# Two transformer blocks on one core: where the roots of the variances are taken, and what Pool does first in a stage

## The reference

```python
x = x + jnp.tanh(g_xattn[0]) * _L0_xattn_ref(_layernorm(x), ctx_512, ...)   # 16 heads over 361 latents, rotary
x = x + jnp.tanh(g_ffn[0])   * _L0_ffn_ref(_layernorm(x), ...)              # weights -1/0/1, rows quantised to 8 bits
x = x + jnp.tanh(g_xattn[1]) * _L1_xattn_ref(_layernorm(x), ctx_512, ...)   # causal, 16 heads
x = x + jnp.tanh(g_ffn[1])   * _L1_ffn_ref(_layernorm(x), ...)              # 7 routed experts (top 2) and a shared one

def _layernorm(x, axis=-1, eps=1e-05):
    m = jnp.mean(x, axis=axis, keepdims=True)
    v = jnp.var(x, axis=axis, keepdims=True)
    return (x - m) / jnp.sqrt(v + eps)
```

## Time and profile before

| | |
|---|---|
| median of 3 runs (lowest, highest) | 1941.34 us (1939.52, 1941.47) |
| the profiled execution | 1943.23 us, of which span 1941.4 us |
| granted PE clock, mean | 0.973 |
| PE busy | 1772.2 us, 91% |
| DVE busy | 1318.7 us, 68% |
| ACT busy | 913.6 us, 47% |
| Pool busy | 599.5 us, 31% |
| stage starts in the trace (first instruction) | 1033.88, 1214.70 and 1448.75 us |

### The profile page before, as it was taken

One profiled execution on the slowest core, in us unless ns is written; L12 is line 12 of the kernel. 1 busy time (PEld: TensorE's weight loads), 2 busy tenths in 40 slices (PEclk: granted clock), 3 DMA queues, 4 the chain that ended last, 5 costly groups with the idle time before them and its releaser, 6 DMA issues. The chain is left out here.

```text
span 1941.4 us, 30474 instructions
## 1 busy us (share of the span) xinstructions
PE 1772.2 (91%) x10896; PEld 1408.2 (73%) x10910; DVE 1318.7 (68%) x2912; ACT 913.6 (47%) x2005; POOL 599.5 (31%) x582
## 2 busy tenths in 40 slices
PE   5899999999899999999996998799978989999997
PEld 4677887778777887778773544566655878888896
DVE  6677677776687778887777896477666633444564
ACT  3544445433543445434543554555544324555563
POOL 5332222331633122321211131232231454343353
PEclk9899999999999999999998999799989999999999
DMA  5022112210121222222205111000005167787773
GB/s 212 17 89 86 55 48 73 89 60 33 62 83 37 97 77 71 71 97 85 77 17 206 36 40 39 25 1 2 1 14 178 57 191 220 239 279 269 236 238 77
DMA packets 49671, 188.50 MB, mean 97 GB/s; under 512 B 7388, under 2 KB 11612, under 8 KB 38260
## 3 DMA queue, kind: packets, MB, share of 16 engines
q1 hardware_dynamic: 39396, 166.86, 24.0%
q0 software_dynamic: 9840, 19.70, 5.6%
q10 hardware_dynamic: 288, 0.00, 0.0%
HBM read 158.29 MB, written 28.24 MB: 96 GB/s over the span
## 5 line engine op out<-in xcount | busy, mean ns | idle before, releaser
L437 POOL TENSOR_TENSOR la_q_roped<-la_q_roped 128x400 f32<-128x400 f32 x128 | 134.7, 1074 | 655.8 <-DVE la_q_roped L968 655.8
L861 ACT ACTIVATE la_probs<-banks,la_minus_max 100x361 f32<-100x361 f32 x256 | 144.7, 565 | 176.6 <-DVE la_minus_max L1079 176.6
L968 DVE TENSOR_TENSOR la_q_roped<-banks,la_rope_q 128x400 f32<-128x400 f32 x384 | 198.0, 566 | 35.4 <-PE banks L552 26.6
L606 PEld LDWEIGHTS banks<-identity,la_probs 100*121 100x121 f32 x768 | 111.8, 185 | 79.4 <-DVE la_probs L1086 54.0
L1086 DVE TENSOR_SCALAR la_probs<-la_probs,la_rsum 100x361 f32<-100x361 f32 x256 | 153.9, 601 | 9.1
L645 PE MATMUL banks<-la_ctx_parts,la_wout_high 128*128 128x416 f32 (+3 forms) x512 | 157.9, 360 | 2.2 <-DVE residual L1020 1.9
L606 PE MATMUL banks<-identity,la_probs 100*121 100x100 f32 x768 | 128.2, 276 | 31.3 <-DVE la_probs L1086 18.9
L1079 DVE TENSOR_REDUCE la_minus_max<-banks 100x1 f32<-100x361 f32 x256 | 134.8, 526 | 29.9 <-PE banks L597 27.8
L617 PE MATMUL banks<-la_probs_t,la_kv_rows 121*128 121x200 f32 x768 | 152.4, 334 | 0.0
L2370 DVE TENSOR_TENSOR ex_weights_low<-ex_raw_weights,ex_weights_high 128x2048 fp32r<-128x2048 f32 x39 | 89.4, 2292 | 90.1 <-ACT ex_weights_high L2254 90.1
L879 ACT COPY la_probs_t<-banks 121x300 f32<-121x300 f32 x256 | 104.8, 409 | 64.0 <-PE banks L606 63.7
(11 more groups left out here) (378 smaller groups left out, 5017.1 us busy)
## 6 DMA issues: line engine op xcount, KB each, us to landing
ex_raw_weights<-w_exp SPq DMA_DIRECT2D x39, 1024.0 KB
la_weights<-w_pack SPq DMA_DIRECT2D x15, 1856.0 KB, 8.4
residual<-w_exp SPq DMA_DIRECT2D x24, 1024.0 KB
la_kv_turned<-w_ffn SPq DMA_DIRECT2D x30, 384.0 KB
la_rope_k<-w_ffn SPq DMA_DIRECT2D x30, 384.0 KB, 3.4
qf_sign_weights<-ffn_signs SPq DMA_DIRECT2D x3, 2048.0 KB, 8.0
ffn_signs<-la_ffn_signs SPq DMA_DIRECT2D x30, 192.0 KB, 2.1
out<-ex_block_out POOLq DMA_DIRECT2D x13, 256.0 KB
```

The lines of the kernel that those rows point to most:

```text
L437: pool.tensor_tensor(roped[:, h, 0, c, :], roped[:, h, 0, c, :], roped[:, h, 1, 1 - c, :], ALU.add).then_inc(b_add, 1)
L606: mm = pe.transpose(ps[0:LC, T_BANK, c * S:(c + 1) * S], prob[:, j % 4, c * LC:(c + 1) * LC], core.ident[0:S, 0:S])
L861: act.activation(prob[:, s % 4, 0:L], ps[0:S, s % 2, 0:L], ACT.Exp, bias=nmax[:, s % 4:s % 4 + 1], accum_out=sums[:, s % 4:s % 4 + 1]).the ...
L968: dve.tensor_tensor(roped[:, h, v, c, :].rearrange("p (b s) -> p b s", b=GB), ps[:, B_BANKS[k % 2], 0:NT].rearrange("p (b s) -> p b s", b=GB),
```

## The change

In words. (1) Stage 1: in the last pair (n = 15) ACT takes the roots of tiles 0 to 5, and DVE runs the six steps before the pair's slots. (2) Stage 2 starts without them: Pool's first `norm` waits for nothing. The table load of `root(lo, PT, ...)` now stands behind the first quantisations. (3) Stage 2, tile 10 (`FIRST_ROOT`): DVE aggregates batches 0 to 3, ACT takes their roots between two tiles, and DVE runs the six steps in tile 11. (4) Stage 3 starts with Pool's `norm` of batches 0 and 1, ahead of the constants. The roots of batches 4 to 11 stand in ACT's list between the rounding of x3 and the copies of k0, and their statistics in DVE's list behind x3. (5) Stage 3, slots 60 to 62 (`NEXT_AT`): DVE aggregates batches 0 to 11 of the new `x`, ACT takes the roots, DVE runs the six steps. (6) Stage 4 starts with `row_norm(0)` and `row_norm(2)` on Pool, ahead of its memsets, and only batches 12 to 15 have their roots here, in ACT's list at t = 2.

```diff
@@ latent_attention, ACT, pair(n)
                     high(n, 3)
+                    if n == RUNS - 1:
+                        act.wait_ge(x_var, B + TILES0)
+                        act.activation(core.std_all[:, 0:TILES0], core.mv_all[:, 0:TILES0, 1], ACT.Sqrt,
+                                       bias=core.eps[:, 0:1]).then_inc(x_std, 1)
@@ latent_attention, DVE, pair(n)
                     rope(n, 3, 0)
+                    if n == RUNS - 1:
+                        norm_rstd_dve(dve, core, x_std, x_rstd, range(TILES0), 3, True)
                     for s in slots(n):
@@ quantised_ffn, Pool, norm(t)
-                    pool.wait_ge(rstd, 6 if t < core.packed[1][0] else 12)
+                    if t >= core.packed[1][0]:
+                        pool.wait_ge(rstd, 6)
@@ quantised_ffn, ACT
-                root(0, lo, 0)
                 act.wait_ge(consts, 2)
...
                     scaled(t)
+                    if t == FIRST_ROOT:
+                        act.wait_ge(b_var, GB)
+                        act.activation(core.std[:, 0:GB], core.mv[:, 0:GB, 1], ACT.Sqrt,
+                                       bias=core.eps[0:S, 0:1]).then_inc(std, 1)
@@ quantised_ffn, DVE
-                norm_rstd_dve(dve, core, std, rstd, range(lo), 0, True)
...
                         add(t - 1)
+                    if t == FIRST_ROOT:
+                        dve.wait_ge(n_bn, PT - lo + 1 + GB)
+                        for b in range(GB):
+                            dve.bn_aggr(core.mv[:, b, :], core.stats[:, b, :]).then_inc(b_var, 1)
+                    if t == FIRST_ROOT + 1:
+                        norm_rstd_dve(dve, core, std, rstd, range(GB), 1)
                     h_quantise(t)
@@ causal_attention, Pool
+                norm(0)
+                norm(1)
                 pool.memset(mask[:], 0.0).then_inc(mask_zero, 1)
...
-                pool.wait_ge(rstd, 6)
...
-                for t in range(GB + 2):
+                for t in range(2, GB + 2):
                     norm(t)
@@ causal_attention, ACT
-                root(0, LATE)
                 act.wait_ge(consts, 7)
...
                 for k in range(NF):
                     front(0, k, k)
+                    if k == GB - 1:
+                        root(GB, LATE, LATE - GB)
...
+                    if s == NEXT_AT + 1:
+                        root(0, LATE, B - GB + LATE)
@@ causal_attention, DVE
+                for k in range(GB):
+                    front(0, k, k)
+                for t in range(GB, 2 * GB):
+                    spread(t)
                 dve.wait_ge(core.rows_in[2], 16 * GB)
                 for t in range(LATE - GB, LATE):
                     stats(t)
                 dve.wait_ge(late_bn, GB)
-                for t in range(LATE):
+                for t in range(2 * GB, LATE):
                     spread(t)
-                norm_rstd_dve(dve, core, std, rstd, range(LATE))
-                for k in range(NF):
-                    front(0, k, k)
+                norm_rstd_dve(dve, core, std, rstd, range(GB, LATE))
                 for s in range(SLOTS):
                     if s < ITEMS:
                         less_max(s)
+                    if s == NEXT_AT:
+                        dve.wait_ge(n_bn, LATE)
+                        for t in range(LATE):
+                            spread(t)
+                    if s == NEXT_AT + 2:
+                        norm_rstd_dve(dve, core, std, rstd, range(LATE), 2)
@@ expert_ffn, ACT
-                norm_stats_act(act, core, ns, range(B))
-                act.wait_ge(ns.rstd, 6)
                 row_norm(1)
                 row_norm(3)
                 for t in range(0, B, 2):
+                    if t == 2:
+                        norm_stats_act(act, core, ns, range(B - GB, B))
                     if t + 5 < B:
+                        if t + 5 >= B - GB:
+                            act.wait_ge(ns.rstd, 6)
                         row_norm(t + 5)
@@ expert_ffn, DVE
-                for t in range(B):
+                for t in range(B - GB, B):
                     dve.bn_aggr(core.mv[:, t, :], core.stats[:, t, :]).then_inc(ns.var, 1)
-                norm_rstd_dve(dve, core, ns.std, ns.rstd, range(B))
                 for t in range(1, B, 2):
                     turned(t)
+                    if t == 3:
+                        norm_rstd_dve(dve, core, ns.std, ns.rstd, range(B - GB, B))
@@ expert_ffn, Pool
+                row_norm(0)
+                row_norm(2)
                 pool.memset(bd[:], 0.0).then_inc(bias_zero, 1)
...
-                pool.wait_ge(ns.rstd, 6)
```

More of the change, by code:

```diff
@@ L1205, in quantised_ffn @@
         consts, var, std, rstd = sem("consts"), sem("mean_var"), sem("std"), sem("rstd")
-        n_bn = sem("x_stats")
+        n_bn, b_var = sem("x_stats"), sem("batch_mean_var")
+        FIRST_ROOT = 10
         n_done, n_max, n_scale, n_inv, n_mul, n_q = (sem(n) for n in (
@@ L1338, in _, with root @@
             def _(act):
-                def root(lo, hi, earlier):
-                    if earlier:
-                        act.wait_ge(var, earlier)
+                def root(lo, hi, tiles):
+                    act.wait_ge(var, tiles)
                     act.activation(core.std_all[:, lo:hi], core.mv_all[:, lo:hi, 1], ACT.Sqrt,
@@ L1483, in _ @@
                     dve.bn_aggr(core.mv_all[0:n, t, :], core.stats_all[0:n, t, :]).then_inc(var, 1)
-                norm_rstd_dve(dve, core, std, rstd, range(lo, PT), 1, True)
+                norm_rstd_dve(dve, core, std, rstd, range(lo, PT), 0, True)
                 for t in range(PT):
@@ L1582, in causal_attention @@
         LATE, LATE_AT = B - GB, 4
+        NEXT_AT = 60
         ITEMS = B * KC
@@ L1623, in _, with norm @@
             def _(pool):
+                def norm(t):
+                    if t >= 2:
+                        pool.wait_ge(x_t, t - 1)
+                    if t >= GB:
+                        pool.wait_ge(rstd, 12 if t >= LATE else 6)
+                    pool.tensor_scalar(xn[:, t % 2, :], core.x[:, t, :], core.rstd[:, t:t + 1],
+                                       core.nmr[:, t:t + 1], ALU.mult, ALU.add).then_inc(normed, 1)
+                norm(0)
+                norm(1)
                 pool.memset(mask[:], 0.0).then_inc(mask_zero, 1)
@@ L1636, in _ @@
                     pool.tensor_copy(maskb[:, h, :], mask[:]).then_inc(consts, 1)
-                pool.wait_ge(rstd, 6)
-                def norm(t):
-                    if t >= 2:
-                        pool.wait_ge(x_t, t - 1)
-                    if t >= LATE:
-                        pool.wait_ge(rstd, 12)
-                    pool.tensor_scalar(xn[:, t % 2, :], core.x[:, t, :], core.rstd[:, t:t + 1],
-                                       core.nmr[:, t:t + 1], ALU.mult, ALU.add).then_inc(normed, 1)
                 def normalise(j):
@@ L1813, in high, with root @@
                                    scale=core.gates[:, 1:2]).then_inc(m_high, 1)
-                def root(lo, hi):
-                    act.wait_ge(var, hi)
+                def root(lo, hi, batches):
+                    act.wait_ge(var, batches)
                     act.activation(core.std[:, lo:hi], core.mv[:, lo:hi, 1], ACT.Sqrt,
                                    bias=core.eps[0:S, 0:1]).then_inc(std, 1)
-                root(0, LATE)
                 act.wait_ge(consts, 7)
@@ L1836, in _ @@
                     if s == LATE_AT + GB:
-                        root(LATE, B)
+                        root(LATE, B, B - GB)
+                    if s == NEXT_AT + 1:
+                        root(0, LATE, B - GB + LATE)
                     if s >= MIX_AT and (s - MIX_AT) % KC == 0 and (s - MIX_AT) // KC < B:
@@ L2679, in _, with row_norm @@
             def _(pool):
+                def row_norm(t):
+                    if t >= XR:
+                        pool.wait_ge(rows_out[t % XR], 16 * (t // XR))
+                        pool.wait_ge(x_t, t - XR + 1)
+                    if t >= B - GB:
+                        pool.wait_ge(ns.rstd, 6)
+                    pool.tensor_scalar(xn(t), core.x[:, t, :], core.rstd[:, t:t + 1],
+                                       core.nmr[:, t:t + 1], ALU.mult, ALU.add).then_inc(normed[0], 1)
+                row_norm(0)
+                row_norm(2)
                 pool.memset(bd[:], 0.0).then_inc(bias_zero, 1)
@@ L2685, in _ @@
                 pool.memset(tab[:, :, 1:2].bitcast(F32), 0.0).then_inc(consts, 1)
-                pool.wait_ge(ns.rstd, 6)
-                for t in range(0, B, 2):
-                    if t >= XR:
-                        pool.wait_ge(rows_out[t % XR], 16 * (t // XR))
-                        pool.wait_ge(x_t, t - XR + 1)
-                    pool.tensor_scalar(xn(t), core.x[:, t, :], core.rstd[:, t:t + 1],
-                                       core.nmr[:, t:t + 1], ALU.mult, ALU.add).then_inc(normed[0], 1)
+                for t in range(4, B, 2):
+                    row_norm(t)
```

## The result

The changed kernel took 1943.72 us (median of 16 runs, 1940.14 to 1947.22), the kernel before 1939.75 us in the runs beside it (16 runs, 1937.4 to 1941.47). The ratio is 1.0018, 95% interval 1.0011 to 1.0025: some 3.5 us slower (2.1 to 4.9), just inside the 0.2% that the prediction called no change, and inside its range. (One run of a later experiment, the root behind k1, took 2666.65 us at a granted clock of 0.603 and is left out of its ratio.) The profiled execution took 1943.58 us with a span of 1941.4 us, which is also the span of the profiled execution before. So two spans say nothing here; the places have to be compared one by one, each from a mark that the edit doesn't move.

What follows compares the result with a forecast made beforehand. PE was busy 91% of the span, so only its waits, above all at three stage starts, could pay. Six terms summed to +1.45 us; on the median of 1941.34 that gave 1942.8 us, range 1938.0 to 1946.5.

Steps and rivals of the forecast that it cites:

- term 3: Stage 2, tile 10 to 11: ACT's load, root, load delay silu and PE waits 1.35 us; +1.5 us, bounds 1.2 and 2.9.
- term 5: Stage 3, slots 60 to 62: DVE's aggregations and six steps delay the last sums; +2.2 us, bounds 1.2 and 3.6.
- term 1: Last pair of stage 1: DVE's six steps delay the first maximum and all passes on; +1.2 us, bounds 0.4 and 1.3.
- term 2: Start of stage 2: Pool 2.6 us earlier, but PE waits for up weights; -1.8 us, bounds -1.0 and -2.6.
- Term 4: Start of stage 3: rows come earlier, but ACT's root holds k0's copies; -0.95 us, bounds -0.6 and -3.2.
- term 6: Start of stage 4: PE's transposes three us earlier, but SP's DMA queue moves only 0.7; -0.7 us, bounds -0.4 and -3.0.
- Rival D: New standstills in stage 2, before q0 and in the last slots put PE at 1.2 GHz; cost 2.5, 1945.3 us; chance 0.10.
- A: Starts of stages 2, 3 and 4 give all they promise, 8.8 us against costs of 4.9; 1937.4 us; chance 0.14.
- B: Added DVE work in stage 1's last pair and slots 60 to 62 is covered; sum -0.35, 1941.0 us; chance 0.10.
- C: Tile 10 and slot 61: a table switch holds ACT longer than its row; +5.7, 1947.0 us; chance 0.07.
- signs of being wrong: k0 copied before 1226, a gap over 0.1 us between an exp and the load behind it, or a shorter stage 3.

Runs made afterwards that it cites:

- The first experiment: Kernel before with only the root and six steps in stage 1's last pair and stage 2 without them; ratio to the kernel before 1.0002 (0.9993 to 1.0011).

## Why the prediction was right, and where its terms were off

Five to nine traces have each edit and five to seven don't; TensorE's clock makes single traces differ by one or two microseconds at some places, so means are compared. A trace counts as with an edit where that stands as in the changed kernel. The root ahead of the scaling counts as without in term 3, the work behind the last sums as without in term 5; for terms 1, 2 and 4 traces with a moved version are left out. Stage 3 is counted from Pool's first instruction.

The total was right, and in part by luck. Forecast were +1.45 us and measured +3.5, near the upper end of what the forecast allowed (-1 to +3.5). The absolute time, 1942.8 against 1943.72, looks closer than that because the kernel before ran at 1939.75 us and not at the 1941.34 that the sum was added to. The places and waits were right in all six terms; what the sum lacked is the clock in terms 2 and 5, and that the gain of term 6 doesn't last. The sizes of terms 2, 4, 5 and 6 were too favourable, by 0.85, 0.25, 0.7 and 0.8 us at the latest marks of the table, and term 3 came out 0.8 us cheaper than forecast.

| term | mark to mark | without | with | measured | predicted |
|---|---|---|---|---|---|
| 1 | rank copy of the last pair to stage 2 | 50.69 (5 traces) | 51.91 (6) | +1.2 | +1.2 |
| 2 | start of stage 2 to first scaling | 24.40 (5) | 23.83 (6) | -0.6 | -1.8 |
| 2 | ... to the fourth scaling | 59.37 (5) | 58.42 (6) | -0.95 | |
| 3 | scaling of tile 10 to that of 11 | 11.35 (7) | 12.87 (7) | +1.5 | +1.5 |
| 3 | scaling of tile 10 to stage 3 | 36.62 (7) | 37.32 (7) | +0.7 | |
| 4 | start of stage 3 to first exp | 31.63 (5) | 30.62 (7) | -1.0 | -0.95 |
| 4 | ... to the maximum of slot 60 | 210.68 (5) | 209.94 (7) | -0.7 | |
| 5 | maximum of slot 60 to stage 4 | 21.43 (5) | 24.35 (7) | +2.9 | +2.2 |
| 6 | start of stage 4 to the gate copy | 29.17 (5) | 28.58 (9) | -0.6 | -0.7 |
| 6 | ... to the third block's copy on ACT | 65.09 (5) | 65.40 (9) | +0.3 | |
| 6 | ... to the end of the span | 492.1 (5) | 492.2 (9) | +0.1 | |

(The first experiment is left out of term 1: its 53.40 has some 1.5 us more from a stretch at 0.83 of the clock, 990 to 1000 us.) With the latest mark of each term, the sum is 1.2 - 0.95 + 0.7 - 0.7 + 2.9 + 0.1 = +3.25 us. Measured were +3.5 (2.1 to 4.9), predicted +1.45. The agreement is loose: from the scatter of the traces I estimate a standard error of 1.1 us for the sum. Terms 1 and 5 and the first marks of terms 2, 3 and 4 are clear of that scatter; the later marks of terms 2, 3 and 4, and all of term 6, are not, or barely.

**Term 1** was right in size and reason. ACT's load and root cost nothing: from the rank copy of the pair before to this one are 45.7 us with and without them. All of DVE's part passed on, and it was avoidable: the last slot hides it.

**Term 2** was mis-sized. The step that failed is "From 1046.82 the three column products up0, gate1, up1 take until 1050.8 as before". They start behind a standstill of PE of 2.69 us, and run at 1.2 GHz: in the window below (columns as above) the granted clock is 0.50, and a product takes 0.43 us until 1052.1 instead of 0.216. The stage starts at that level in the kernel before too, but there it rises 15.4 us into the stage, here 17.9. So DVE's second product comes at 1052.59, which is 1052.10 counted from the start of the stage before, and not at 1050.85. The other traces agree: without the edit the clock rises at 14.4 to 15.8 us, with it at 16.8 to 18.8, and the earliest rise has the earliest first scaling (23.15 us), the latest the latest (24.49). With the weights in halves it rises at 10.4 and 12.2 us. The weights are the first limit, as predicted, and that clock the second. Rival D named this mechanism.

```profile
1040.00:1050.00 10.00, 5.85 (x22) 2.44 (x24) 7.55 (x28) 6.33 (x9) 0.77 (x1) 0.50 1.01 429
```

**Term 3** was right: load, root, load at the row's durations, PE's wait 1.33 us for a predicted 1.35. The bound above it (2.9) wasn't touched. By the start of stage 3 it is +0.7 on the mean: the tail behind the last scaling is 11.7 us long in three of the seven traces with the gap and in none of the seven without, else 13.0 to 14.6. Whether PE's standstill in tile 10 or chance spares the clock later was not tried.

**Term 4** was right in its account: q0 1.25 us earlier, 2 us of PE's standstill ahead of it, and 0.3 us lost by the later mark. What it missed is that q0's clock varies: in 3 of 7 traces with the edit it is at full speed at once (first exp at 29.8), in 4 it isn't (31.2 to 31.3), with the same wait of 1.99 us ahead of it. The three are the same three traces whose stage 2 ends early in term 3. From the scaling of tile 10 to the maximum of slot 60 they take 245.1 to 245.2 us; the three others with both edits in their first place take 248.4 to 249.4, and the five with neither 246.4 to 248.0. So the clock moves this stretch by 4 us, and the two edits together move its mean by 0.2 (247.1 against 247.3).

**Term 5** was mis-sized, and it is the term that a profile of one execution hid. DVE's part is right: 2.08 us for a predicted 2.15. The rest is the clock of the output product behind it. Without added work ahead of the last sums it is undisturbed in three traces of five (20.6 to 21.05 us) and low in two (22.3 and 22.55). With the work it is low in all seven, and in both kernels with one engine's work alone. If work and clock had nothing to do with each other, all three undisturbed traces would fall among those five in 3% of cases (10 of 364). So the work very likely brings the low clock; by what way is not shown, as PE's waits do not go with it. The profiled execution of before is one of the two low ones: its window reads 6.50 us and a clock of 0.74, so its comparison with the one of after showed 1.7 us where the mean is 2.9.

```profile
1433.15:1439.65 6.50, 5.29 (x20) 3.79 (x21) 2.62 (x7) 1.90 (x4) 1.71 (x2) 0.74 0.00 0
```

**Term 6** was right in its mechanism and wrong as a gain of the kernel. SP issues the rows 3.1 us into the stage in all nine traces with the edit and 3.85 in the five without, and the DMA of the gate matrix at 22.2 us on the mean for 22.9: the 0.7 us of the sum. At the gate copy the means still differ by 0.6, but single traces lie between 28.3 and 30.6 without and 27.7 and 29.6 with. Nothing of it is left 65 us into the stage, where traces of either kind spread from 63.4 to 66.3. The step that failed is that the weights landing earlier was taken for a gain of the whole stage. Why ACT's and DVE's next weights take it back was not separated.

**The rivals.** A (stage starts give all) fell: the weights of stage 2 did not shift, those of stage 4 by 0.7 us and not 3, and k0 was held. B fell: the DVE work costs its full length. C fell: between a load and what stands on either side of it, where nothing else is waited for, are 0.01 to 0.02 us in the changed kernel, in slots, tile and stage starts alike, so the drain that the Trainium skill gives in "ScalarE: Activation LUTs" (What ACT_TABLE_LOAD costs) isn't there. Its rule (Table sets: the hidden batching unit) to batch by set still has a point here: the two loads are the 2.56 of the 2.86 us that hold silu in tile 10. D is the one that happened beside the forecast, with 0.85 us in term 2 and 0.7 in term 5, against the 2.5 that it was given.

**The signs.** Of the signs of being wrong that the prediction named, one is there: stage 3 is shorter in the profiled execution after (233.5 us from stage start to stage start) than in the one before (234.1). The other traces don't bear it out: five with edits (4) and (5) both in their first place have 233.5 to 235.0, mean 234.3, and the two with neither 234.1 and 231.4. A sign smaller than the 2.7 us between two traces of the same code was a weak one.

## What to carry to other kernels

Work that leaves a stage start should go where its new engine waits for the same chain anyway: ahead of the long scaling, behind the last sums, in the last slot of the pair. There the same edits, with the weights of stage 2 in halves besides, went from 0.2% slower to some 0.3 or 0.4% faster. Look at the granted clock of the work behind each place too: at the lower level it made terms 2 and 5 dearer by 0.85 and 0.7 us than the sum had them. And before a difference of 2 us is read from two traces, look at the same mark in traces of kernels that share the place: the one profiled execution of before held a dip that hid 1.2 of the 2.9 us of the costliest term.

## What the runs showed of the hardware

The granted clock fell at the same few places in many traces and not in others of the same code: in tiles 1 and 2 of stage 2, ahead of the scaling of tile 9 (the step from there to tile 10 takes 10.3 or 11.7 us), behind the last tile, and at q0. In between, from tile 3 to tile 8, the tiles of stage 2 repeat at 11.47 to 11.49 us in all fourteen traces. Runs of one kernel lie 4 to 13.5 us apart, and dips of 1.0 to 1.6 us each are what I found to differ between their traces at the edited places. Time also differs where nothing was edited: one of ACT's copies of the ranks in stage 1, ahead of every edit, stands at 856.4 to 860.9 us in the fourteen traces.

The step from tile 8 to 9 takes 17.04 to 17.15 us in every trace, 5.6 more than its neighbours, in both kernels. No experiment looked into it; it is larger than all that this change moved.
